# Where the length-only part of a patch attention is computed: within the first attention, or at the front of a later one

## The reference

```
x = x + L0_xattn(ctx, layernorm(x), masks)      # 8 heads, masked
x = x + L0_ffn(layernorm(x))                    # 4 routed rounds
x = x + L1_xattn(layernorm(x), ctx)             # 16 heads, no mask, keys: ctx rows then x rows
x = x + L1_ffn(layernorm(x))
x = x + L2_xattn(layernorm(x), ctx, lens)
...
```

```
bidx = cumsum(patch_lens) - 1
plug = clip(cumsum(boundary_mask) - 1, 0, plen - 1)
s[p] = sum over j <= p of exp(-DT * (p - j)) * KEEP * rmsnorm(ctx[j], g_init)
z    = s[plug] + b
```

## Time and profile before

| | us |
|---|---|
| median of 3 runs | 1276.37 (1274.05 to 1276.74) |
| profiled execution, its own time | 1281.73 |
| its span in the profile | 1280.1 |
| PE busy | 1111.4 (87%) |
| DVE busy | 781.1 (61%) |
| ACT busy | 683.4 (53%) |
| POOL busy | 395.9 (31%) |

### The profile page before, as it was taken

One profiled execution on the slowest core, in us unless ns is written; L12 is line 12 of the kernel. 1 busy time (PEld: TensorE's weight loads), 2 busy tenths in 40 slices (PEclk: granted clock), 3 DMA queues, 4 the chain that ended last, 5 costly groups with the idle time before them and its releaser, 6 DMA issues.

```text
span 1280.1 us, 18272 instructions
## 1 busy us (share of the span) xinstructions
PE 1111.4 (87%) x6234; PEld 773.2 (60%) x6234; DVE 781.1 (61%) x1914; ACT 683.4 (53%) x1613; POOL 395.9 (31%) x612
## 2 busy tenths in 40 slices
PE   3677899999859998778899999967999799998777
PEld 2346677777613344656677777745777567675665
DVE  5754687788667672668766677664111366666464
ACT  3253567666515575366677778752343266666022
POOL 5311112111121110236466676672000144444200
PEclk8686899999966799888989999986999899999979
DMA  5411000000050400300000000214000100000000
GB/s 208 100 49 58 1 1 13 1 1 1 1 161 20 170 21 2 132 0 1 1 1 1 1 1 17 116 46 192 1 1 1 67 1 1 1 2 2 1 1 17
DMA packets 26572, 45.10 MB, mean 35 GB/s; under 512 B 3536, under 2 KB 23792, under 8 KB 25200
## 3 DMA queue, kind: packets, MB, share of 16 engines
q1 hardware_dynamic: 23936, 41.57, 9.4%
q10 hardware_dynamic: 2544, 2.36, 0.6%
HBM read 36.94 MB, written 6.82 MB: 34 GB/s over the span
## 4 chain that ended last, share of the span: by engine, by line
PE 68%; DVE 13%; ACT 8%; issue 5%; POOL 2%; DMA 2%; SPq 2%; ACTq 0%; DVEq 0%; POOLq 0%
PE psum L1179 7%; PE psum L1554 7%; PE psum L1169 5%; PE psum L919 5%; PE psum L929 4%; ACT region_d L1620 3%; PE psum L2187 3%; PE psum L409 2%; PE psum L2164 2%; PE psum L2131 2%; PE psum L2148 2%; PE psum L2126 2%; PE psum L1541 2%; PE psum L365 2%; PE psum L1591 2%
## 5 line engine op out<-in xcount | busy, mean ns | idle before, releaser
L1554 PE MATMUL psum<-gated_parts 128*128 128x512 f32 x768 | 198.6, 413 | 16.6 <-DVE region_d L1725 14.7
L1554 PEld LDWEIGHTS psum<-gated_parts 128*128 128x128 f32 x768 | 142.5, 193 | 68.5 <-DVE region_d L1725 32.6
L1794 POOL TENSOR_TENSOR region_d<-region_d 128x256 f32<-128x256 f32 x128 | 101.9, 796 | 121.4 <-DVE region_d L1725 120.1
L1254 ACT ACTIVATE rounds_work<-psum,region_c 128x512 f32<-128x512 f32 x128 | 87.0, 689 | 59.3 <-PE psum L1169 59.2
L787 DVE TENSOR_REDUCE work<-psum 128x1 f32<-128x512 f32 x128 | 82.1, 686 | 34.4 <-PE psum L365 32.8
L1725 DVE SCALAR_TENSOR_TENSOR region_d<-psum,ctx,region_d 128x128 f32<-128x128 f32 x256 | 71.8, 343 | 45.3 <-ACT region_d L1620 41.7
L1620 ACT ACTIVATE region_d<-psum,gated_work 128x128 f32<-128x128 f32 x256 | 75.2, 438 | 44.9 <-issue 26.1
L1179 PE MATMUL psum<-parts,split 128*128 128x512 f32 x384 | 97.6, 404 | 0.0
L1169 PE MATMUL psum<-parts,split 128*128 128x512 f32 x384 | 94.2, 396 | 0.0
L1324 DVE TENSOR_TENSOR parts<-rounds_work,parts 128x1024 fp32r<-128x1024 f32 x64 | 77.5, 1223 | 20.1 <-POOL parts L1410 17.4
L1725 DVE SCALAR_TENSOR_TENSOR region_d<-psum,gated_work,region_d 128x128 f32<-128x128 f32 x256 | 71.3, 344 | 29.1 <-ACT region_d L1620 19.0
(11 more groups left out here) (377 smaller groups left out, 2263.3 us busy)
## 6 DMA issues: line engine op xcount, KB each, us to landing
region_a<-in_l1v SPq DMA_DIRECT2D x1, 4096.0 KB, 15.4
region_b_last<-in_l1o SPq DMA_DIRECT2D x1, 4096.0 KB, 12.4
region_a<-in_l2f SPq DMA_DIRECT2D x1, 4096.0 KB, 13.4
region_b_last<-in_l3f_small SPq DMA_DIRECT2D x1, 4096.0 KB, 19.7
region_a<-in_l3f SPq DMA_DIRECT2D x1, 2080.0 KB, 7.6
region_c<-in_l0f SPq DMA_DIRECT2D x1, 2076.0 KB, 12.3
region_c<-in_l3x SPq DMA_DIRECT2D x1, 2048.0 KB, 8.0
ctx_parts<-front_work SPq DMA_DIRECT2D x6, 256.0 KB, 3.6
```

Of the source, the lines that this page charges most:

```text
L1254: act.activation(H[g % 2][:, f, :], bank[f], ACT.Gelu_apprx_tanh, bias=W("b1")[:, (g % E) * FT + f:(g % E) * FT + f + 1]).then_inc(h_ready ...
L1554: ins = pe.matmul(bank[2 * (n % 2) + c], src[a][:, t * P:(t + 1) * P], weights[b][:, piece(c)], start=m == 0, stop=m == len(PASSES) - 1)
L1794: pool.tensor_tensor(tile[:, 0:2, :], tile[:, 0:2, :], tile[:, 2:4, :], ALU.add).then_inc(k.pool_chain, 1)
```

## The change

Only `pe_counts` and `dve_bounds` stay in the first attention; they are called ahead of the steps. `bound`, `upto16`, `before` and `least` get a place of their own (`patch_kept`, 264 words of a partition) that lives on to stage 2, and WORK is shorter by as much. The rest is called by the unmasked attention: the plugs on PE ahead of the transposes, the decays on ACT ahead of the copies of xnT, rows and keep on DVE between the splits of the first and the second pair, the sums on PE between the second pair's first subtraction and the first step, the take on DVE ahead of the first row maxima. POOL's split now waits for the first exp of the first attention.

```diff
@@ tensor
         if masked:
             ahead.pe_ends(pe)
+        else:
+            pe.wait_ge(k.x_tiles, NT * number)
+            ahead.pe_plugs(pe)
         k.norm.tensor(pe, use, k.xn)
...
         if masked:
             pe.wait_ge(*biased.at(4))
+            ahead.pe_counts(pe)
         else:
             pe.wait_ge(*rest.at(first_of(3)))
             pe.wait_ge(*part.at(first_of(3)))
+            ahead.pe_sums(pe)
...
-                if masked and s == 1:
-                    pe.wait_ge(ahead.z_ready, 2)
+                if s == 1:
+                    pe.wait_ge(*((ahead.bound_ready, 1) if masked else (ahead.z_ready, 2)))
...
-            if masked and i == 0:
-                ahead.pe_counts(pe)
-            if masked and i == 1:
-                ahead.pe_plugs(pe)
-            if masked and i == 3:
-                ahead.pe_sums(pe)
@@ scalar
+        if not masked:
+            ahead.act_decays(act)
         k.norm.scalar(act, use, k.xnT)
...
-            if masked and i == 1:
-                ahead.act_decays(act)
@@ gpsimd
-            pool.wait_ge(ahead.z_ready, 2)
+            pool.wait_ge(*p2_exp.at(1))
             split.gpsimd(pool)
@@ vector
+            if pair == 0 and not masked:
+                ahead.dve_rows(dve, chain)
+                ahead.dve_keep(dve)
         if masked:
             ahead.dve_hits(dve, chain)
             ahead.dve_statistics(dve, chain)
+            ahead.dve_bounds(dve)
+        else:
+            ahead.dve_take(dve)
...
-            if masked and i == 0:
-                ahead.dve_bounds(dve)
-                ahead.dve_rows(dve, chain)
...
-            if masked and i == 2:
-                ahead.dve_keep(dve)
-            if masked and i == 4:
-                ahead.dve_take(dve)
```

More of the change, by code:

```diff
@@ L218, in packed_attention @@
         cp = [k.carve(BF16, T) for _ in range(3)]
+    else:
+        ahead.carve_later()
     q_dram, k_dram = k.q_dram[number], k.k_dram[number]
@@ L1833, in __init__ @@
         self.ones = k.carve(F32, P)
-        self.upto16 = k.carve(BF16, TPB, S)
+        self.upto16 = k.patch_kept[:, 0:S].bitcast(BF16).rearrange("p (t s) -> p t s", t=TPB)
         self.ones16 = k.carve(BF16, 2)
@@ L1837, in __init__ @@
         self.part_id = k.carve(F32, TPB)
-        self.before = k.carve(F32, TPB)
-        self.least = k.carve(F32, TPB)
+        self.before = k.patch_kept[:, S:S + TPB]
+        self.least = k.patch_kept[:, S + TPB:S + 2 * TPB]
         self.lens, self.ends, self.wrap = (k.carve(F32, NT) for _ in range(3))
         self.hit = k.carve(BF16, NT, S)
-        self.bound = k.carve(BF16, NT)
-        self.decay = [k.carve(F32, B, S) for _ in range(TPB)]
-        self.u = k.carve(F32, NT, D)
+        self.bound = k.patch_kept[:, S + 2 * TPB:S + 2 * TPB + NT // 2].bitcast(BF16)
         self.z = k.mask_bc[:, :].rearrange("p (t d) -> p t d", t=NT)
@@ L1858, in __init__, with carve_later @@
         self.z_ready = k.sem("patch_z_ready")
+    def carve_later(self):
+        self.decay = [self.k.carve(F32, B, S) for _ in range(TPB)]
+        self.u = self.k.carve(F32, NT, D)
     def pool_consts(self, pool):
@@ L2720, in build @@
         if last_stage >= 3:
-            stages.append(packed_attention(k, "l1x", 2, 16, 8, 4, False, 1e-5, k.weight_views("l1x", L1X)))
+            stages.append(packed_attention(k, "l1x", 2, 16, 8, 4, False, 1e-5, k.weight_views("l1x", L1X), ahead))
         k.open_gated()
@@ L2789, in __init__ @@
         self.mask_bias = sb("mask_bias", [1, T], BF16)
+        self.patch_kept = sb("patch_kept", [P, PATCH_KEPT])
         self.ctx_work = {"stats": sb("ctx_stats", [P, NT, 6])[:, :, :], "mean_var": sb("ctx_mean_var", [P, NT, 2])[:, :, :],
@@ L2863, in open_rounds @@
         self.work_extent.close()
-        self.work_extent.enter_context(self.nc.sbuf_tensor("kept_for_l1x", [P, REGION_B], F32))
+        self.work_extent.enter_context(self.nc.sbuf_tensor("kept_for_l1x", [P, REGION_B - PATCH_KEPT], F32))
         parts = 2 * PARTS + T + HALF
@@ L2867, in open_rounds @@
         self.parts = [flat[:, 0:PARTS], flat[:, PARTS:2 * PARTS], flat[:, 2 * PARTS:]]
-        self.work = self.work_extent.enter_context(self.nc.sbuf_tensor("rounds_work", [P, WORK - REGION_B - parts], F32))
+        self.work = self.work_extent.enter_context(self.nc.sbuf_tensor("rounds_work", [P, WORK - REGION_B + PATCH_KEPT - parts], F32))
     def open_later(self):
@@ L2943 @@
 PARTS = 5120
-WORK = REGION_B + 18090
+PATCH_KEPT = S + 2 * TPB + NT // 2
+WORK = REGION_B + 18090 - PATCH_KEPT
 WEIGHTS = {"l0x": ("D", 0), "l0f": ("C", 0), "l1x": ("D", 1290), "l1f": ("D", 2320), "l1v": ("A", 0), "l1o": ("B", 0), "l2x": ("E", 0),
```

## The result

The changed kernel took 1279.79 us (median of 8 executions, 1277.82 to 1295.87) where the kernel before, on the same chip, took 1275.49 (8 executions, 1273.69 to 1279.12). The ratio is 1.0062, 95% interval 1.0031 to 1.0092: slower by some 0.6%, where no change was forecast. (The two medians alone are 4.30 us or 0.34% apart; the three executions of the changed kernel above 1290 us weigh in the ratio.) The time lies within the range given, and the move does not match the forecast.

The account below looks back on a forecast made before the run. The first attention's path was taken to run through plugs, decays, keep, sums and take; -4.1 + 5.0 - 0.75 = +0.15 us on the profiled 1281.73, so 1276.5 us against a median of 1276.37, range 1271 to 1281.

Parts of the forecast that it names:

- The landing of the maxima: First attention: first unit's maxima land behind the loads, second-pass product at 48.3 instead of 52.66, 4.36 us; bounds 47.3 and 49.5.
- rival C: First attention: maxima land late or L778 wait longer for POOL; -4.1 becomes -2.5, 1278 us; chance 0.48 together with no change.
- the turn: First attention: next product (L422) after the first second-pass product, at 55.0 instead of 59.16, behind values, bias add and L778.
- -4.1 us: First attention: gain once plugs, decays, keep and sums are gone, next product at 55.0 instead of 59.16; bounds -6.3 and -2.6.
- +5.0 us: Start of the unmasked attention: the moved work puts the first reduction at 375.5 instead of 370.52; bounds +2.2 and +7.2.
- the 3.0 of the forecast: Unmasked attention: lateness of q's first half after the late xnT copies, taken near the middle of 2.0 and 3.7 us.
- the 3.7: Unmasked attention: lateness in us of q's first half if k and q both run at the low clock.
- the sums' own duration: Unmasked attention: sums on PE taken at 5.22 us, ending at 374.7 and deciding the first reduction; bounds 3.6 and 6.8.
- The table load: Unmasked attention: the load before the first exp goes, since exp's table is in place, -0.75 us; one of 1.28 precedes the decays' Exp.
- The middle stages lose and gain nothing.: Stages between: no change in time, since the sums' result is read only in the fifth stage.
- A (the clock carries over): Unmasked attention: sums leave PE's clock high for the first passes, saving at most 5 us, 1271.5 us; chance 0.28.
- B (the first attention loses its warm clock): First attention: without the sums PE stays at the low clock and nothing is given back, 1280.6 us; chance 0.24.

Follow-up runs that it names:

- e3: Kernel before with plugs, decays, rows, keep, sums and take left out in every stage, at its old addresses; 1274.92 us, ratio 0.9966.
- e1: Changed kernel with patch_kept padded from 264 to 384 words, so the work space keeps its offset modulo 512 bytes; 1277.97 us, ratio 0.9981.
- e4: Changed kernel run again unchanged, on the chip of e1 to e3; 1280.05 us, ratio 1.0016.
- e16: Changed kernel with patch_kept of 272 words instead of 264, order of loads unchanged; 1280.95 us, ratio 1.0033.
- e7: e3 with the work space shifted by 32 bytes; 1279.38 us.
- e8: e1 with the first unit's maxima issued by SP ahead of the loads of images 2 and 3; 1268.40 us, ratio 0.9923.
- e14: Kernel of e8 run again, beside e13 and e15 on one chip; 1268.72 us, ratio 0.9927.
- e9: Kernel before with the first unit's maxima issued ahead of the loads of images 2 and 3; 1276.08 us, ratio 1.0008.
- e2: Kernel before with an unused 8-word tile that shifts the work space by 32 bytes; 1277.84 us, ratio 0.9988.
- e10: e8 without the padding (patch_kept of 264 words, maxima first); 1272.96 us, ratio 0.9978.
- e15: Kernel of e10 run again, beside e13 and e14 on one chip; 1280.64 us, ratio 1.0023.
- e13: e8 with patch_kept of 272 words instead of 384; 1271.75 us, ratio 0.9943.
- e11: e8 without the sums on PE and the take on DVE, and without the fifth stage's wait for them; 1263.80 us, ratio 0.9906.
- e12: e3 with the first unit's maxima issued ahead of the loads, as in e8; 1269.84 us, ratio 0.9947.
- e5: Kernel before, unchanged, for a second profile; 1274.97 us.
- e6: Kernel before, unchanged, for a third profile; 1275.37 us.

## Why the prediction was wrong, point by point

**The landing of the maxima (the step that failed).** The forecast had: "they land behind loads that fill the queues to 47.25: I take 48.3 instead of 52.66." The 47.25 (the end of 25 slices, not 26) was read from a kernel in which the first-pass loads ran at that kernel's pace. In six profiles with the sums out of the way and the old order of loads, the product stood between 50.64 and 56.34, and both ends of the bound (47.3 and 49.5) were too early. Two things are in it. First, the queue: at the addresses of before it stays full to 48.3 and the product comes at 50.64 and 51.45 (e3, e1), 2.3 and 3.2 us past the forecast; with the work space shifted it stays full to between 50.1 and 52.8, and the product comes at 53.1 to 56.3. It never came sooner than 2.3 us after the last full slice, where the forecast had 1.05. Second, the issue: SP, behind its own slower loads, issued the first maxima at 48.14 in the changed kernel's profile and at 46.1 to 46.8 in e4, e16 and e7, where the forecast kept the 44.89 of before (e1 44.72, e3 44.43). e8 and e14 show that the place behind the loads is the cause: in front of them the product comes at 42.4 to 44.3 and the ratio falls by 0.6% against e1. e9 shows that the order by itself, with the sums still there, gives nothing. The forecast had a late landing as rival C, but at a price of 1.6 us (1278), and all of the gain was lost.

**The address (a price that was missing).** That patch_kept's place moves the work space was not in the sum. Packets of the same loads then take longer. Of the step from 47.7% of the queue's window before (7368 packets) to 72.5% after (7339), some 9 points are there at the old addresses too (58.1 and 56.5% in e1 and e3); the shift adds another 7 in e4 and e16 and 15 in the changed kernel's first profile. In the kernel before it does not reach the time (e2: 0.9988); the change takes away just that cover. Padded, the changed kernel has a ratio of 0.9981 (0.9956 to 1.0007), which is the "no change" that was forecast; unpadded, 1.0062, 1.0016 and, at 272 words, 1.0033. Only part of the price is on the first product's path: e10 and e15 have the product at 43 to 45 and still lose 4.6 and 11.9 us to e8 and e14. Where the rest goes is open. From the turn to the end of the first attention the three kernels that were shifted and had the maxima first (e10, e13, e15) took 60.8 to 61.1 us, with the granted clock at 0.50 until 64; e14 and e11 took 57.7 and 57.4, with the clock high from 58, but e8, in place as well, took 61.3. From the third stage's first exp to its end e10 and e15 take 4.4 us more than e8 and e14 (127.6 against 123.2, means of two). That the shift brings a late rise of the clock there is not shown: it rose 14 us or more behind that exp in before, e1 and e3, which are unshifted, as in e15, e16 and the changed kernel, and about 4 us behind it in e10 and e13, which are shifted.

**"-4.1 us" in the first attention.** What follows the product was right: 6.83 us to the turn in the changed kernel, 6.83 in e4, 6.84 in e1 (forecast 6.7), with the mask beside POOL. At the old addresses something was given back: the first attention ended at 113.7 and 115.8 (e3, e1) where three profiles of before have 118.0 on average. With the shifted work space it ended at 122.7, 115.2 and 118.8 in the changed kernel, e4 and e16, on average 118.9, and at 118.3 in e7. Nothing was given back there.

**"+5.0 us" at the front.** The order of the steps and what decides at the end were right; measured 5.9 against the earlier trace rows, and 26.60 to 26.78 us after x in all nine profiles with the sums there. That the start of the sums was off by 0.1 us is luck, since two terms were off and cancelled. The clock was high and not low when x was ready, so the plugs took 1.05 us instead of 1.95, and the second copy of xnT ended 7.54 us after x, 1.2 us later than before and not 2.2. And k and q of the first half both ran at the low clock, where the forecast took a middle: together the two make the first ACT operation on q 3.04 us late (10.99 us after x), the 3.0 of the forecast. The Trainium skill ("TensorE: Matmul & The Clock Gate", Part 4: PE-mode transpose) says that transposes do not count as busy time for the gate. The forecast read this as both running low, and in this trace they did (0.50 in 360 to 364); the 3.7 is not reached because the plugs were early. Whether transposes that do not count are the reason is not shown, since PE also stood idle for 1.5 us ahead of k. What was mis-sized is the sums' own duration, 6.34 instead of 5.22: they were taken with the clock of the first attention, where it was low for 2.8 us of the 5.22, and here it was low for about four fifths. The forecast's bounds for them (3.6 and 6.8) do not follow from its own row either, as 2.8 us low and 2.4 high make 3.8 and 7.6. The arrival of the first pass's data without them was taken 1.1 us too late (e11), which shows only when the sums are gone.

**The table load.** Of the 5.9 us the first exp sees 4.95, so 0.9 come back (forecast 0.75), and a load of 1.28 us stands between the decays, as forecast. Nothing beyond the load is to be seen: the next ACTIVATE begins at 357.44, 0.02 us after the load's end. The Trainium skill ("ScalarE: Activation LUTs", What ACT_TABLE_LOAD costs) has 2.66 us for a switch with its drain, which again no row here shows.

**"The middle stages lose and gain nothing."** The rounds took 230.0 to 230.9 us with the moved work in the third stage and 231.4 to 232.5 without it, a gain of about 1.5 us that the forecast did not have. Its cause stays open; it is not POOL's earlier split, which e3, e7 and e12 have too.

**The terms together.** By the means of three profiles each (changed, e4, e16; before, e5, e6), the first attention gives +0.9 us instead of -4.1, the front +5.9 instead of +5.0, the table load -1.1 instead of -0.75 and the rounds -1.6 instead of nothing. That is +4.1, beside the 4.30 between the medians. So near a fit is partly luck, since the stretch from the first exp to the end differs by more than that from one execution to the next.

**The rivals.** A (the clock carries over): it did not. The clock was high when the sums ended, had fallen by 382, and was 0.50 in 390 to 400, where the first exp stands, as the forecast's own objection said. Where it was high in 390 to 400 (e14), it was in e11 too, which has no sums to carry it. B (the first attention loses its warm clock) had the right size by chance, 1280.6. Its sign did appear, the low clock in the middle of the first attention. Changed kernel, then the kernel before:

```profile
66.00:72.00 6.00, 6.00 (x37) 3.19 (x36) 3.89 (x7) 3.83 (x6) 5.84 (x4) 0.50 0.01 1
```

```profile
66.00:72.00 6.00, 3.31 (x29) 2.03 (x28) 5.54 (x10) 2.18 (x4) 2.25 (x1) 1.00 0.01 1
```

But its price did not: from the turn to the end the first attention took 59.5, 55.2 and 57.8 us in the changed kernel, e4 and e16, and 59.0, 57.9 and 59.0 in before, e5 and e6. What was lost was lost ahead of the turn. A slower outcome by way of the DMA queue was there only as a mild case (C), since its price was read from a trace in which something else hid the queue.

**A version that beats both.** The change with patch_kept padded to 384 words and the first maxima issued ahead of two loads: 0.9923 (0.9897 to 0.9950) and 0.9927 (0.9896 to 0.9957) of the kernel before. It needs all three: maxima first alone gives 1.0008 (e9), the padded change alone 0.9981 (e1), and the change with the maxima first but no padding 0.9978 and 1.0023 (e10, e15).

## What to carry to other kernels

When something that the path waited for is removed, what it waits for next must be read from the queue as it will be, not as it was. Here small transfers stood behind bulk loads, and issuing them first, at the old addresses, gave more (0.6%) than the change had cost. Any new buffer moves the ones behind it; keep their place (a padding of 480 bytes here) before the rest is judged. And PE work that is moved to a place where the clock is low must be priced at the low clock: the sums took 6.34 us there and not 5.22. Last, a term that comes out right can be two errors: compare every step of a sum with the trace, not only its end.

## What the runs showed of the hardware that was not expected

The time that a DMA packet takes depends on where in a partition its data go. With the same loads in 24 to 60 us, the queue's packets took 47.7 to 49.9% of the window in three profiles of the kernel before and 63.8% with the work space 32 bytes further on; in e8's order 40.2 to 44.0% in five profiles in place, 50.2% at 1088 bytes, 52.2 and 58.0% at 1056. Even in place, the changed kernel's share is higher (58.1%, and 56.5% in e3); why is open, and e8's order brings it below that of before.

Executions of one kernel differ by more than the change is worth, along with the granted clock: the 35 of the kernel before that stood beside e1 to e4 go from 1271.81 us at a mean of 0.919 to 1289.08 at 0.900. One kernel had a ratio of 0.9978 on one chip and 1.0023 on another (e10, e15), and e12, with less work than e11, took 6 us more, at mean clocks of 0.907 to 0.918 against 0.916 to 0.918.
